# Sliding-window attention on one core: mixing with the values is issued behind the next half's scores, and the row maxima ahead of the output split

## The chip, the cores and the metric

The kernel runs on one core of a Trainium2 chip. The metric is the device time of one execution in microseconds (us). The core has a matrix engine (TensorE: PE for its matmuls, PEld for its weight loads), VectorE (DVE), ScalarE (ACT), GpSimd (POOL) and SyncE (SP), which issues the DMAs. Each engine runs its own list of instructions in order, and they meet only through semaphores.

## The reference, cut to what matters

The input is x (4 x 1024 x 512). First comes a banded cross-attention with a context (here "the band"), then two layers of a transformer block:

```python
for l in range(2):
    h = shift_token(x)
    q, k, v = split(h @ wqkv[l])               # 8 heads of 64
    q, k = rotary_xpos(l2norm(q) * qs, l2norm(k) * ks)
    o = local_attention(q, k, v)               # a row sees at most the 256 rows before it
    x = x + o @ wo[l]
    x = x + gated_ffn(layernorm(shift_token(x)))
```

For each row, local_attention takes the scores with the keys in reach, their maximum, the exponentials, divides by their sum, and multiplies with the values. All of it is in float32, which TensorE gets by splitting an operand into a rounded ("high") and a remaining ("low") part and making three products.

## The kernel before

The rows are cut into 32 tiles of 128 (8 per batch entry). The phases are the band, attention of layer 0, its FFN, attention of layer 1, its FFN. The change touches only the attention phase.

That phase is one software pipeline, written out by hand in five programs, one for each engine. Each has a loop `for s in range(TILES + 3)` and inside it two halves, `for d in (0, 1)`. In step s the tile t = s - 2 has its scores made (four heads in each half), tile s - 3 ("tail") is finished, tile s is projected to q, k and v, and tile s + 1 is turned (transposed). A tile reaches over 1, 2 or 3 tiles of keys: one for the first tile of a batch entry, two for the second, three for the other six (`reach`, L126).

TensorE's list for an inner step is, with the lines of its functions:

- d = 0: `scores(t, 0)` (L1074, matmuls L1094, six for each of two pairs of heads); the projection to the values (`project`, L976, matmuls L1000, twelve); `turn_probabilities(t - 1, 1)` (L1107, transposes L1116, twelve); eight more matmuls of the projection; `turn_h(s + 1)` (L1042, four transposes L897); `mix(t - 1, 1)` (L1120, L1133, 24 matmuls where the reach is three).
- d = 1: `scores(t, 1)`; ten matmuls of the projection; `turn_probabilities(t, 0)`; `project_out(tail)` (L1138, twelve matmuls L901 to L903); `turn_q` and `turn_k` of tile t + 1 (L1056, L1064); the last six matmuls of the projection; `mix(t, 0)`.

A half's probabilities are therefore turned one half later than its scores, and mixed at the end of that half. Three things hold the order together:

- PSUM banks. The four banks of `quad` are shared: the scores of the even pair of heads use banks 2 and 3, those of the odd pair banks 0 and 1. `turn_h` and `turn_q` write bank 1 and `turn_k` writes bank 0. So the odd pair in half d = 1 waits until h of tile s + 1 has been taken out of bank 1, which is L1088:

```python
w.wait_ge(S("hT_low"), base + min(t + 3 + d, TILES))
```

- Operands. `scores` starts with waits for both parts of q and k of its tile (L1080, L1081: qT_low, kT_low). These are made from PSUM by ACT (high, `copy` at L1354, called from `split_q`, `split_k`, `split_h`) and then DVE (low, L1718, functions of the same names).
- The lists of ACT and DVE. DVE takes the maxima (`maximum`, L1878, L1884), which also move the scores out of PSUM, scales the probabilities (`divide`, L1863), splits h, q and k, and splits the mixed output (`split_out`, L1921). ACT takes the exponentials (`probabilities`, L1528, L1533), copies turned probabilities (`copy_turned`, L1564), and makes the first part of the splits. In d = 1 both have `split_out(tail)` ahead of the maxima and of the exponentials. `turn_probabilities` waits at L1111 until all four maxima of the half just scored are taken, since it writes the same banks. `project_out` waits for oT_low, DVE's `split_out`.

POOL turns q and k by the rotary tables and scales some probabilities. In steps 12, 14, 16 and 18, DVE also has an extra scaling between `split_q` and `split_k` (`early_scale`, L2013, L2016), and in many steps POOL, ACT and DVE prepare parts of the FFN's weights (part_low, part_high).

Of the kernel before, what the change touches and what calls it, by code (L numbers as in the profile page):

```python
# [214 lines left out]
def build(nc, x, ctx, mask, wqkv, q_scale, k_scale, wo, ln_g, ln_b, w1, b1, w2, b2, consts, out):  # L215
# [676 lines left out]
    def tensor_program(e):  # L892
# [146 lines left out]
        def attend(l):  # L1039
# [80 lines left out]
            def mix(t, d):  # L1120

                n = base + t
                k, tiles, _, _ = reach(t)
                w.wait_ge(S("v_rows"), n + 1)
                w.wait_ge(S("oT_low"), n)
                if t == 0 and d == 0:
                    w.wait_ge(S("hT_low") if l else S("x1"), base + 2 if l else TILES)
                for turned, p in enumerate(duo(d)):
                    wait_copied(n, d, turned + 1)
                    for j in range(tiles):  # L1130
                        for i, half in enumerate(half_of):
                            h = 2 * p + i
                            ins = e.matmul(banks[5][half, p * P:(p + 1) * P],  # L1133
                                           A.v_rows[:, k - tiles + 1 + j, h * HD:(h + 1) * HD],
                                           A.probT[p % 2][:, i, j * P:(j + 1) * P], start=j == 0, stop=j == tiles - 1)
                    ins.then_inc(S("lmix"), 1)
# [14 lines left out]
            for s in range(TILES + 3):  # L1151
                t, tail = s - 2, s - 3
                live, ended = 0 <= t < TILES, 0 <= tail < TILES
                inside = 1 < s < TILES
                if s == 0:
                    turn_h(1)
                    project(l, 0, 0, 12)
                if s == 1:
                    project(l, 1, 12, 24)
                    turn_h(2)  # L1160
                    project(l, 1, 24, 36)
                    turn_q(0)
                    project(l, 1, 0, 6)
                    turn_k(0)
                    project(l, 1, 6, 12)
                for d in (0, 1):
                    turned = (t, 0) if d else (t - 1, 1)
                    mixing = 0 <= turned[0] < TILES
                    if live:
                        scores(t, d)  # L1170
                    if inside:
                        project(l, s, PROJECTED[d][0], PROJECTED[d][1])
                    if (s, d) == (TILES, 0):
                        project_out(tail - 1, 0)
                    if (s, d) == (TILES, 1):
                        turn_unit(l, 0)
                        turn_unit(l, 1)
                        project_out(tail, 0)
                    if (s, d) == (TILES + 1, 0):
                        turn_unit(l, 4)  # L1180
                        turn_unit(l, 5)
                    if (s, d) == (TILES + 1, 1):
                        up_first(l, 0, 0)
                    if mixing:
                        turn_probabilities(*turned)
                    if (s, d) == (2, 0):
                        turn_h(3)
                    if inside and d == 0:
                        project(l, s, PROJECTED[0][1], PROJECTED[0][2])
                    if d == 0 and 3 <= s < TILES - 1:  # L1190
                        turn_h(s + 1)
                    if (s, d) == (TILES, 0):
                        project_out(tail - 1, 1)
                    if (s, d) == (TILES + 1, 0):
                        turn_unit(l, 6)
                    if (s, d) == (TILES + 2, 0):
                        project_out(tail - 1, 1)
                    if d and ended and s not in (TILES - 1, TILES):
                        project_out(tail, 0)
                    if d and ended and s not in (TILES - 1, TILES + 1):  # L1200
                        project_out(tail, 1)
                    if d and 2 <= s <= TILES:
                        turn_q(s - 1)
                        turn_k(s - 1)
                    if (s, d) == (TILES, 1):
                        turn_unit(l, 2)
                        turn_unit(l, 3)
                    if inside and d:
                        project(l, s, PROJECTED[1][1], PROJECTED[1][2])
                    if mixing:  # L1210
                        mix(*turned)
                    if (s, d) == (TILES + 2, 0):
                        up_second(l, 0, 0)
                        up_third(l, 0, 0)
# [135 lines left out]
    def scalar_program(e):  # L1350
# [165 lines left out]
        def attend(l):  # L1516
# [56 lines left out]
            for s in range(TILES + 3):  # L1573
                t, tail = s - 2, s - 3
                live, ended = 0 <= t < TILES, 0 <= tail < TILES
                for d in (0, 1):
                    turned = (t, 0) if d else (t - 1, 1)
                    if l and (s, d) == (0, 0):
                        split_h(l, 1)
                    if d == 0 and rotated_tile(s) is not None and (l or s):  # L1580
                        square(l, rotated_tile(s))
                    if d and ended:
                        split_out(tail)
                    if live:
                        for h in range(4 * d, 4 * d + 4):
                            probabilities(t, h)
                    if (s, d) == (TILES + 1, 0):
                        split_unit(l, 4)
                        split_unit(l, 5)
                    if (s, d) == (TILES + 1, 1):  # L1590
                        keep_first(l, 0, 0)
                    if 0 <= turned[0] < TILES:
                        copy_turned(*turned)
                    if (s, d) == (TILES, 1):
                        split_unit(l, 0)
                        split_unit(l, 1)
                    if (s, d) == (TILES + 1, 0):
                        split_unit(l, 6)
                    if d == 0 and s < TILES and s != 1:
                        keep_v(s)  # L1600
                    if l and (s, d) == (0, 0):
                        e.activation(small[:, 0, 0:16], half_power[:, :], ACT.Exp).then_inc(S("half_power"), 1)
                    if d == 0 and 1 <= s < TILES - 1:
                        split_h(l, s + 1)
                    if l and (s, d) in ((0, 0), (1, 0)):
                        out_split_begin(l, 2 * s)
                        out_split_begin(l, 2 * s + 1)
                    if l and (s, d) == (2, 0):
                        attend_split_finish(l, 3)
                    if d and 1 <= s <= TILES:  # L1610
                        split_q(s - 1)
                        split_k(s - 1)
                    if (s, d) == (1, 1):
                        keep_v(1)
                    if prepared_item(s, 1) is not None:
                        if d:
                            round_parts(l, prepared_item(s, 1))
                        else:
                            round_sums(l, prepared_item(s, 1))
                    if (s, d) == (TILES, 1):  # L1620
                        split_unit(l, 2)
                        split_unit(l, 3)
                    if (s, d) == (TILES + 1, 0):
                        down_split_begin(l, 0)
                    if (s, d) == (TILES + 2, 0):
                        down_split_finish(l, 0)
                    if (s, d) == (TILES + 2, 1):
                        gate(l, 0, 0)
                        split_u(l, 0, 0)
                        down_split_begin(l, 1)  # L1630
# [77 lines left out]
    def vector_program(e):  # L1708
# [145 lines left out]
        def attend(l):  # L1854
# [66 lines left out]
            def split_out(t):  # L1921
                n = base + t
                w.wait_ge(S("oT_high"), n + 1)
                low(A.oT[:, 1, :], banks[5], A.oT[:, 0, :], S("oT_low"))
# [9 lines left out]
            for s in range(TILES + 3):  # L1934
                t, tail = s - 2, s - 3
                live, ended = 0 <= t < TILES, 0 <= tail < TILES
                for d in (0, 1):
                    early = early_tile(s) if d else None
                    if d and ended:
                        split_out(tail)  # L1940
                    if live:
                        for h in range(4 * d, 4 * d + 4):
                            maximum(t, h)
                    if (s, d) == (0, 0):
                        split_h(1)
                    if l and (s, d) == (0, 0):
# [488 lines left out]
```

## Time and profile before

| what | value |
|---|---|
| median of 3 runs | 2904.82 us (2904.49 to 2905.25) |
| the profiled execution | 2905.07 us |
| its span, first to last instruction | 2903.3 us |
| PE busy / PEld busy | 2872.9 us (99%) / 2526.7 us (87%) |
| DVE / ACT / POOL busy | 2075.6 us (71%) / 1340.3 us (46%) / 1328.4 us (46%) |
| mean granted TensorE clock | 1.000 |

The band takes about the first 220 us. Attention of layer 0 lies at about 220 to 850 us, that of layer 1 at about 1575 to 2210 us; the rest is FFN. A row of the timeline gives start, duration, engine, line, operation and tiles; equal neighbours are merged and counted with x; in brackets stands the idle time of the engine ahead of it and what ended it. A matmul's end is modelled and reaches over the start of the next, so for PE starts are compared with starts.

### The profile page before, as it was taken

How to read it: one execution, taken by the hardware profiler on the slowest of the kernel's cores; microseconds unless marked ns; L12 is line 12 of the kernel's file. 1: busy time of each engine (PE TensorE's matmuls, PEld its weight loads, DVE VectorE, ACT ScalarE, POOL GpSimd, SP SyncE). 2: the span in 40 equal slices, each digit the busy share in tenths (PEclk: the TensorE clock that was granted, in tenths of full speed). 3: DMA queues.
4: the chain of work that ended last, by engine and by line, in shares of the span. 5: the costliest groups of instructions: out<-in, count | busy, mean ns of one | idle time of the engine just before them, and what ended most of it. 6: DMA issues, size and time to landing. Idle time of an engine off the chain costs nothing. (4 is left out here: it accounts for less than half of the span.)

```text
span 2903.3 us, 53018 instructions
## 1 busy us (share of the span) xinstructions
PE 2872.9 (99%) x20256; PEld 2526.7 (87%) x20256; DVE 2075.6 (71%) x4135; ACT 1340.3 (46%) x2807; POOL 1328.4 (46%) x1406
## 2 busy tenths in 40 slices
PE   9999999999999999999999999999999999999999
PEld 7887888888889999999998887888888999999998
DVE  8987777776677666766657777776676766666765
ACT  7875556555554222222235555555555332222221
POOL 7767677776642211122105676766662222222221
PEclk9999999999999999999999999999999999999999
DMA  6753233322147777777783223332217777777775
GB/s 219 238 186 102 95 102 106 115 95 81 32 163 294 276 280 261 268 266 257 258 312 117 95 92 110 110 106 88 62 56 288 272 281 272 279 283 280 282 272 186
DMA packets 184897, 547.02 MB, mean 188 GB/s; under 512 B 26678, under 2 KB 82490, under 8 KB 162116
## 3 DMA queue, kind: packets, MB, share of 16 engines
q1 hardware_dynamic: 184500, 543.57, 52.9%
q8 instruction: 161, 2.64, 0.4%
q14 instruction: 92, 0.75, 0.1%
q10 hardware_dynamic: 144, 0.07, 0.0%
HBM read 447.11 MB, written 93.70 MB: 186 GB/s over the span
## 5 line engine op out<-in xcount | busy, mean ns | idle before, releaser
L1246 PE MATMUL quad<-fhT_f,slot_f 128*128 128x256 f32 (+1 forms) x2088 | 595.4, 285 | 0.2 <-DVE sums_f L2061 0.2
L1247 PE MATMUL quad<-fhT_f,slot_f 128*128 128x256 f32 (+1 forms) x2088 | 590.7, 283 | 0.0
L1248 PE MATMUL quad<-fhT_f,slot_f 128*128 128x256 f32 (+1 forms) x2088 | 590.5, 283 | 0.0
L1246 PEld LDWEIGHTS quad<-fhT_f,slot_f 128*128 128x128 f32 (+1 forms) x2088 | 392.9, 188 | 0.4 <-DVE sums_f L2061 0.4
L1248 PEld LDWEIGHTS quad<-fhT_f,slot_f 128*128 128x128 f32 (+1 forms) x2088 | 393.1, 188 | 0.0
L1247 PEld LDWEIGHTS quad<-fhT_f,slot_f 128*128 128x128 f32 (+1 forms) x2088 | 393.1, 188 | 0.0
L1665 ACT ACTIVATE gate_f_raw<-gate_f_raw,bias_f 128x512 f32<-128x512 f32 (+1 forms) x176 | 127.2, 722 | 552.2 <-DVE gate_f_raw L2084 552.2
L1533 ACT ACTIVATE lprob<-lprob,small 128x384 f32<-128x384 f32 (+2 forms) x512 | 288.5, 565 | 179.0 <-DVE small L1884 179.0
L2172 POOL TENSOR_SCALAR stats<-stats 128x1 f32<-128x1 f32 x64 | 35.6, 557 | 692.1 <-DVE stats L2024 691.3
L2289 POOL TENSOR_TENSOR turned_qk<-with_cos,with_sin 128x256 f32<-128x256 f32 x252 | 186.7, 761 | 337.6 <-DVE with_sin L1908 243.9
L1000 PE MATMUL bank_pair<-wqkv_h,hT 128*128 128x512 f32 x992 | 318.7, 402 | 0.0
L1884 DVE CUSTOM_DVE_ANT_0 lprob<-quad,far 128x384 f32<-128x384 f32 (+2 forms) x512 | 228.8, 503 | 74.6 <-PE quad L1094 74.6
L2280 POOL TENSOR_SCALAR lprob<-lprob,small 128x384 f32<-128x384 f32 (+2 forms) x192 | 238.7, 1250 | 23.7 <-DVE small L1869 23.7
L2346 POOL TENSOR_TENSOR res_f<-res_f,bias_f 128x512 f32<-128x512 f32 x63 | 89.2, 1416 | 282.5 <-DMA res_f<-stream 282.5
L2095 DVE SCALAR_TENSOR_TENSOR u_f<-sums_f,bias_f,gate_f_raw 128x512 f32<-128x512 f32 (+1 forms) x176 | 147.2, 837 | 95.6 <-ACT gate_f_raw L1665 95.6
L1354 ACT ACTIVATE lprobT<-quad 128x768 f32<-128x768 f32 (+2 forms) x256 | 172.2, 724 | 68.2 <-PE quad L1116 66.7
L1000 PEld LDWEIGHTS bank_pair<-wqkv_h,hT 128*128 128x128 f32 x992 | 177.5, 189 | 29.7
L1000 PE MATMUL bank_pair<-wqkv_l,hT 128*128 128x512 f32 x496 | 201.7, 407 | 0.0
L2207 POOL TENSOR_TENSOR norm<-norm,half_power 128x16 f32<-128x16 f32 x64 | 196.1, 3064 | 5.3
L1116 PEld LDWEIGHTS quad<-ident,lprob 128*128 128x128 f32 x1344 | 151.7, 141 | 32.8 <-DVE small L1884 20.4
L2084 DVE TENSOR_TENSOR gate_f_raw<-quad,sums_f 128x512 f32<-128x512 f32 (+1 forms) x174 | 120.3, 691 | 79.2 <-PE quad L1248 76.3
L1116 PE MATMUL quad<-ident,lprob 128*128 128x128 f32 x1344 | 169.4, 274 | 7.3 <-DVE small L1884 7.2
(296 smaller groups left out, 7344.1 us busy)
## 6 DMA issues: line engine op xcount, KB each, us to landing
slot_f<-parts SPq DMA_DIRECT2D x160, 1792.0 KB, 7.7
slot_f<-parts SPq DMA_DIRECT2D x16, 1190.0 KB, 5.2
s_in<-stream SPq DMA_DIRECT2D x128, 128.0 KB, 2.8
s_res<-stream SPq DMA_DIRECT2D x64, 256.0 KB, 2.8
stream<-a_out SPq DMA_DIRECT2D x64, 256.0 KB, 2.0
res_f<-stream SPq DMA_DIRECT2D x63, 256.0 KB, 7.3
h_in_f<-stream SPq DMA_DIRECT2D x112, 128.0 KB, 5.3
parts<-part_high SPq DMA_DIRECT2D x20, 512.0 KB, 2.6
```

Source lines behind the costliest of these rows:

```text
L1000: ins = e.matmul(bank, A.hT[n % 2][:, i % 2, c * P:(c + 1) * P], (wqkv_l if i == 2 else wqkv_h)[:, c, cols], start=(c, i) == (0, 0), stop= ...
L1116: ins = e.transpose(quad[:, pair_banks(p) + i, j * P:(j + 1) * P], A.prob[p][:, i, j * P:(j + 1) * P], ident[:, :])
L1246: e.matmul(bank[0:n, :], high, row_high, start=c == 0, stop=False)
L1247: e.matmul(bank[0:n, :], high, row_low, start=False, stop=False)
L1248: ins = e.matmul(bank[0:n, :], low, row_high, start=False, stop=c == 1)
L1354: return e.activation(to, source, ACT.Copy)
L1533: e.activation(prob, prob, ACT.Exp, bias=sm[:, h:h + 1], scale=-1.0, accum_out=sm[:, 8 + h:9 + h]).then_inc(S("lprob"), 1)
L1884: e.tensor_tensor_reduce(A.prob[h // 2][:, h % 2, 0:cols], quad[:, pair_banks(h // 2) + h % 2, 0:cols], A.far[:, WIN - cols:], 1.0, BIG, A ...
L2095: e.scalar_tensor_tensor(out=Fm.u[q % 2][0:n, :], in0=flat(Fm.sums[q % 2][0:n, 0:2, :]), scalar=Fm.bias1[0:n, 0, j:j + 1], in1=Fm.gate[q % ...
L2207: e.tensor_tensor(nm[:, 16:32], nm[:, 0:16], half_power[:, :], ALU.pow).then_inc(S("norm_inverse"), 1)
L2280: e.tensor_scalar(prob, prob, sm[:, 16 + 2 * p:17 + 2 * p], None, ALU.mult).then_inc(S("pscaled_pool"), 1)
L2289: e.tensor_tensor(turned[:, :, a:a + h2], cos[:, :, a:a + h2], sin[:, :, b:b + h2], ALU.add).then_inc(S("rotated"), 1)
```

## The change

On TensorE `mix` of both halves of tile t - 1 moves. The first half's, formerly at the end of the half d = 1 of step s, now stands in the half d = 0 of step s + 1 behind that half's scores. The second half's, formerly at the end of d = 0, stands behind the scores of d = 1 of the same step. The functions, waits and buffers are the same. On DVE `split_out` goes from ahead of the four maxima of d = 1 to behind them, and on ACT from ahead of the four exponentials of d = 1 to between the second and the third.

```diff
 # tensor_program, attend
                     mixing = 0 <= turned[0] < TILES
                     if live:
                         scores(t, d)
+                    if ended:
+                        mix(tail, d)
                     if inside:
                         project(l, s, PROJECTED[d][0], PROJECTED[d][1])
...
                     if inside and d:
                         project(l, s, PROJECTED[1][1], PROJECTED[1][2])
-                    if mixing:
-                        mix(*turned)
 # scalar_program, attend
-                    if d and ended:
+                    if d and ended and not live:
                         split_out(tail)
                     if live:
                         for h in range(4 * d, 4 * d + 4):
+                            if h == 6 and ended:
+                                split_out(tail)
                             probabilities(t, h)
 # vector_program, attend
-                    if d and ended:
-                        split_out(tail)
                     if live:
                         for h in range(4 * d, 4 * d + 4):
                             maximum(t, h)
+                    if d and ended:
+                        split_out(tail)
```

## Rows read from the trace of the kernel before

**Rows 1.** The page, busy time of each engine (share of the span, instructions)

```profile
PE 2872.9 (99%) x20256; PEld 2526.7 (87%) x20256; DVE 2075.6 (71%) x4135; ACT 1340.3 (46%) x2807; POOL 1328.4 (46%) x1406
```

**Rows 2.** Busy time by stretch: length, PE, PEld, DVE, ACT, POOL, clock, DMA share, GB/s

```profile
225.00:846.00 621.00, 612.94 (x4517) 501.82 (x4517) 452.44 (x1096) 362.87 (x832) 432.38 (x401) 1.00 0.29 95
1583.00:2209.00 626.00, 619.12 (x4597) 508.23 (x4596) 454.19 (x1094) 366.62 (x834) 425.37 (x393) 1.00 0.29 98
```

**Rows 3.** Waits of PE, whole span: total us, times, longest

```profile
PE quad L1116 <- DVE small L1884: 7.2, 23, 1.3
PE quad L1094 <- DVE hT L1718: 3.2, 10, 0.7
```

**Rows 4.** Timeline, layer 1, from turning h to the scores of d = 1

```profile
1713.95 0.60 PE L897 MATMUL quad<-ident,s_in 128*128 128x128 f32 x4
1714.47 1.53 PE L1133 MATMUL bank<-lprobT,v_rows 128*64 128x128 f32 x24
1714.58 0.60 ACT L1354 ACTIVATE hT<-quad 128x512 fp32r<-128x512 f32 x1 [0.93 <-PE quad L897]
1715.21 0.69 DVE L1718 TENSOR_TENSOR hT<-quad,hT 128x512 fp32r<-128x512 f32 x1 [0.40 <-ACT hT L1354]
1715.93 1.32 PE L1094 MATMUL quad<-kT,qT 64*128 64x384 f32 x12
```

**Rows 5.** Timeline, the same place one batch entry later, mixing of reach one

```profile
1752.67 0.66 PE L1133 MATMUL bank<-lprobT,v_rows 128*64 128x128 f32 x8
1753.25 0.62 PE L1094 MATMUL quad<-kT,qT 64*128 64x256 f32 x6
...
1753.40 0.69 DVE L1718 TENSOR_TENSOR hT<-quad,hT 128x512 fp32r<-128x512 f32 x1
1754.15 0.63 PE L1094 MATMUL quad<-kT,qT 64*128 64x256 f32 x6 [0.28 <-DVE hT L1718]
```

**Rows 6.** Timeline, scores of reach one in d = 1

```profile
1736.67 0.89 PE L1094 MATMUL quad<-kT,qT 64*128 64x128 f32 x12
```

**Rows 7.** Timeline, layer 1, from d = 1 into the next d = 0

```profile
1704.14 0.69 DVE L1718 TENSOR_TENSOR qT<-quad,qT 128x512 fp32r<-128x512 f32 x1 [3.16 <-ACT qT L1354]
...
1704.75 0.68 DVE L1718 TENSOR_TENSOR kT<-quad,kT 128x512 fp32r<-128x512 f32 x1
...
1705.23 1.53 PE L1133 MATMUL bank<-lprobT,v_rows 128*64 128x128 f32 x24
```

**Rows 8.** Timeline, layer 1, the same place after step 32

```profile
2183.96 1.53 PE L1133 MATMUL bank<-lprobT,v_rows 128*64 128x128 f32 x24
...
2185.02 0.68 DVE L1718 TENSOR_TENSOR kT<-quad,kT 128x512 fp32r<-128x512 f32 x1
...
2185.84 1.33 PE L1094 MATMUL quad<-kT,qT 64*128 64x384 f32 x12 [0.35 <-DVE kT L1718]
```

**Rows 9.** Line L2016: min/median/max ns, first and last start

```profile
L2016 DVE SCALAR_TENSOR_TENSOR square<-square,stats,shift x8: 743/748/1211, 434.5 to 1907.3; 128x512 f32<-128x512 f32 x8
```

**Rows 10.** Timeline, the last projection matmul ahead of turned probabilities, d = 0 and d = 1

```profile
1710.57 0.39 PE L1000 MATMUL bank<-wqkv_l,hT 128*128 128x512 f32 x1
1710.80 1.47 PE L1116 MATMUL quad<-ident,lprob 128*128 128x128 f32 x12
...
1719.36 0.39 PE L1000 MATMUL bank_pair<-wqkv_l,hT 128*128 128x512 f32 x1
1719.94 1.53 PE L1116 MATMUL quad<-ident,lprob 128*128 128x128 f32 x12 [0.20 <-DVE small L1884]
```

**Rows 11.** Timeline, layer 1, mixing followed by full-array transposes

```profile
2200.10 1.53 PE L1133 MATMUL bank<-lprobT,v_rows 128*64 128x128 f32 x24
2201.57 1.53 PE L1116 MATMUL quad<-ident,lprob 128*128 128x128 f32 x12
```

**Rows 12.** Timeline, layer 1, the last mixing and the split of its output

```profile
2204.41 1.53 PE L1133 MATMUL bank<-lprobT,v_rows 128*64 128x128 f32 x24
...
2206.61 0.69 DVE L1718 TENSOR_TENSOR oT<-bank,oT 128x512 fp32r<-128x512 f32 x1 [1.41 <-ACT oT L1354]
```

## The prediction

> **What bounds the kernel now.** I began with the page: PE is busy for 99% of the span, no other engine for more than 71% [rows 1]. The busy time by stretch says the same of both attention phases: 612.94 of 621.00 us and 619.12 of 626.00 us, at a granted clock of 1.00 [rows 2]. So TensorE's own list sets the time. A change of order takes away none of its work; it can only remove or make waits. Next I read PE's waits. What this change could remove is small: 7.2 us in 23 waits of the turned probabilities on DVE's maxima. And the second row of the group is a warning: scores already wait for h's split, 10 times, 3.2 us [rows 3]. So the question is what the moved mixing stands between, which only the timeline shows.
>
> **What the mixing hides now, d = 1.** In a full tile (reach three) the list is: turning h at 1713.95, mixing at 1714.47, scores at 1715.93 [rows 4]. Mixing thus takes 1.46 us between starts. Meanwhile ACT copies h (1714.58) and DVE splits it from 1715.21 to 1715.90 [rows 4]; both start within 0.03 us of their input, so this chain cannot be shorter. The odd pair's scores, which write h's bank, start half of 1.32 us after the even pair's, at 1716.59, and find it free. With mixing gone from there, the even pair starts at 1714.47 and the odd pair would at 1715.13. It must wait until 1715.90 and a release. That release took 0.06 us: DVE done at 1754.09, PE at 1754.15 [rows 5]. So 1715.96: a **new stall of 0.83 us**. It isn't paid back, since mixing then follows at its full length. Rows 5 are the natural experiment: mixing has reach one there and hides only 0.58 us (1752.67 to 1753.25), and the odd pair does wait. With it moved, the odd pair starts no earlier and mixing's 0.58 us is added behind. Where the scores have reach one, the odd pair is due after half of 0.89 us [rows 6], so its stall is 0.66 - 0.45 = 0.21 us longer, 1.04.
>
> Count: h is turned with a mixing behind it in steps 3 to 30, 28 in each layer. Of these 4 have the short mixing, 3 the narrow scores (tiles 8, 16, 24), 21 are ordinary: 4 x 0.58 + 3 x 1.04 + 21 x 0.83 = 22.9 us, for two layers **+45.7 us**.
>
> **The next d = 0.** Here scores need k's low part. DVE has it at 1704.75 + 0.68 = 1705.43, and mixing starts at 1705.23 [rows 7]; today its 1.46 us cover this. The release of the first pair took 0.14 us where it was the last thing waited for: 2185.70 to 2185.84 [rows 8]. So scores start at 1705.57 instead of 1705.23, **0.34 us late**. There are 31 such places in a layer, 62. Eight have the extra scaling between q and k, 0.75 us each [rows 9], so 1.09. After step 32 (two places) k comes even after the mixing, which is added in full, 1.46 [rows 8]. 52 x 0.34 + 8 x 1.09 + 2 x 1.46 = **+29.3 us**.
>
> **What it removes.** In d = 1 the turned probabilities wait for the fourth maximum: 0.58 us after the last projection matmul's start instead of 0.23 [rows 10], a loss of 0.35. With maxima first on DVE and 1.46 us of mixing more between scores and turning, this is gone: 23 x 0.35 = **-8 us**. Ends: nothing at all, and 20 us if each of the 23 lost nearly 0.9. I take 8, from the row. Next late behind them would be ACT's copy of the turned probabilities; the mixing that needs it is now later too.
>
> **The moved splits.** DVE's split_out no longer stands ahead of the maxima, and ACT's waits behind two exponentials. What hides this is the ten projection matmuls and the twelve transposes that stand between mixing and project_out, over 3.5 us (ten starts 0.23 apart and 1.47 [rows 10]). Split output is there 2.89 us after mixing's start (2204.41 to 2207.30), of which mixing is 1.46 [rows 12]; two exponentials more fit in the rest. I cost it at nothing. If that cover is gone, it is 1.49 us: 2.89 + 0.06 - 1.46. That happens at the end of each layer: the last mixing now stands directly ahead of project_out, behind two FFN products: 2 x 1.49. In step 32, only eight transposes stand between, two thirds of 1.47 us [rows 10]: 2 x 0.5. Together **+4.0 us**. No DMA moves past another in SP's list, and POOL's list is untouched.
>
> **Switches of the array's shape.** The three kinds of matmul use it whole, by rows (scores) and by columns (mixing). 24 mixings take 1.46 us and 8 take 0.58 [rows 4, 5]; 16 more thus cost 0.88, 0.055 each, and 0.14 us is left for the switch. Mixing ahead of whole-array work takes 1.47 us, 2200.10 to 2201.57 [rows 11], the same as ahead of scores. Scores directly ahead of mixing are nowhere in the trace. Bounds for that one: no switch cost (-0.14) to twice (+0.14), at 128 places -18 to +18 us. I take 0, since the measured pairs agree. The Trainium skill, page "TensorEngine Tiling (Array Packing)", section Key Properties, says that every change of tiling mode drains TensorE. A half has three changes before and three after, so by that rule, too, the estimate is no difference.
>
> **Sum.** 45.7 + 29.3 - 8 + 4 = +71 us on the profiled execution's 2905.07 us, which is 0.25 us above the median of the runs shown: **2976 us**.
>
> **The rivals.**
>
> One handover hurts only. If ACT and DVE come to q and k earlier in d = 1, k's 29 us fall away: 2905 + 46 + 4 - 8 = 2947 us. Against it: ACT and DVE already stood idle ahead of them (3.16 us of DVE before q [rows 7]), so they can't start earlier. Chance 0.06.
>
> DVE comes late. Its split_out now waits for ACT behind two exponentials, and `divide` behind it. If that pushed an instruction of 0.69 us in front of every k, 62 x 0.69 = 43 us more: 3019 us. It decides once the delay exceeds the 3.16 us of idle [rows 7]; I see some 1.5. Chance 0.07.
>
> The other side, faster. The waits on the maxima go, and the handovers stay hidden: 2905 - 8 = 2897 us. This needs h's chain from the start of turning to the free bank, 1.95 us now (1713.95 to 1715.90), to come down to 1.12, at which point the odd pair would wait no more. It consists of 0.60 us of transposes, 0.60 of ACT and 0.69 of DVE with nothing between [rows 4], so I give it 0.03.
>
> The change doesn't do what it says: some other wait already holds the mixing where it is now, 2905 us. But rows 4 show mixing starting 0.52 us after four transposes began, with no wait named. Chance 0.02.
>
> The clock falls. Both phases run at 1.00, though PE idles about 8 us in each [rows 2]. More and longer stalls could bring the granted clock to 1.2 GHz. For a tenth of 1247 us that would be 125 us of work taking twice as long: 3100 us. The Trainium skill, "TensorE: Matmul & The Clock Gate", section HAM oscillation, has a kernel in which TensorE's waits brought its clock down again and again. Those waits were for DMAs, and no run here shows the lower clock. Chance 0.01.
>
> My forecast has the remaining 0.81.
>
> **How the numbers follow.** Range, low end: switch free (-18), a release of 0.06 instead of 0.14 us for k (-5), the removed waits worth 20 instead of 8 (-12): 2976 - 35 = 2941. That takes in the first rival. High end: +18 for the switch, and a few late k's of the second rival's kind, +6: 3000. Left out are 0.07 + 0.03 + 0.02 + 0.01 and some tails of the forecast. A measurement of this kernel can tell about 0.2%, 6 us, from no change. Faster: 0.03. Same: 0.02. Slower: the rest, 0.95.
>
> **What the profile after would show.** Scores of d = 1 split in two groups of six, the second waiting for DVE's hT, in nearly all of steps 3 to 30, both layers: about 56 waits of PE on hT in place of 10. New waits of PE on kT, about 60. None on the maxima ahead of turned probabilities in d = 1. Both attention stretches about 35 us longer, with the same PE work; the band and the FFN unchanged. I am wrong if the odd pair starts less than 1.9 us after h's first transpose, or if the stretches don't grow.

## The result: 2.5% slower, two handovers uncovered

| | median us | runs |
|---|---|---|
| before | 2905.01 | 2904.49 to 2905.25 |
| changed | 2977.69 | 2977.16 to 2979.03 |

The ratio is 1.0251, with a 95% interval of 1.0238 to 1.0263. The forecast was 2976 us. The profiled execution took 2979.03 us, 74.0 us more than that of before.

The changed kernel's page has the same number of instructions on every engine, and a smaller busy share of PE (97%, from 99%); its row of before is [rows 1]:

```profile
PE 2887.0 (97%) x20256; PEld 2531.5 (85%) x20256; DVE 2066.5 (69%) x4135; ACT 1339.4 (45%) x2807; POOL 1337.6 (45%) x1406
```

Busy time by stretch (length, PE, PEld, DVE, ACT, POOL, clock, DMA share, GB/s), the same parts of the work as [rows 2]: 621 us became 658, and 626 became 663. All of the time was lost in the attention phases, 37 us in each.

```profile
225.00:883.00 658.00, 621.81 (x4531) 505.99 (x4530) 449.65 (x1105) 364.14 (x838) 437.03 (x401) 1.00 0.28 90
1620.00:2283.00 663.00, 626.67 (x4600) 511.71 (x4601) 449.78 (x1095) 366.12 (x835) 430.13 (x392) 1.00 0.28 93
```

PE's waits (total us, times, longest), against [rows 3]. The 10 waits on h have become 58. I read the 58 "issue" waits ahead of scores as those for k: the view names nothing for them, but they stand at the places where they were forecast, and in the half d = 0 shown below k lands just ahead of the scores. The waits on the maxima have left the list of PE's longest.

```profile
PE quad L1094 <- DVE hT L1720: 42.2, 58, 0.9
PE quad L1094 <- issue: 21.0, 58, 1.3
PE bank L901 <- DVE oT L1720: 4.7, 4, 1.4
PE quad L1094 <- DVE qT L1720: 3.5, 2, 1.8
```

The timeline of one half d = 1 of the changed kernel, layer 1, against [rows 4]. (DVE's lines are 2 higher than before, L1720 for L1718.)

```profile
1756.43 0.60 PE L897 MATMUL quad<-ident,s_in 128*128 128x128 f32 x4
1756.95 0.79 PE L1094 MATMUL quad<-kT,qT 64*128 64x384 f32 x6
1757.06 0.60 ACT L1354 ACTIVATE hT<-quad 128x512 fp32r<-128x512 f32 x1 [0.94 <-PE quad L897]
1757.69 0.69 DVE L1720 TENSOR_TENSOR hT<-quad,hT 128x512 fp32r<-128x512 f32 x1 [1.91 <-ACT hT L1354]
1758.44 0.79 PE L1094 MATMUL quad<-kT,qT 64*128 64x384 f32 x6 [0.69 <-DVE hT L1720]
...
1759.16 1.53 PE L1133 MATMUL bank<-lprobT,v_rows 128*64 128x128 f32 x24
...
1760.62 0.50 PE L1000 MATMUL bank_pair<-wqkv_l,hT 128*128 128x512 f32 x1
...
1763.06 1.47 PE L1116 MATMUL quad<-ident,lprob 128*128 128x128 f32 x12
```

This is the sequence that was forecast. The even pair starts 0.52 us after h's transposes; the odd pair stops until DVE is done (1757.69 + 0.69 = 1758.38) and starts 0.06 us later. From the first transpose to the odd pair it is 2.01 us, and 2.01 was forecast. ACT and DVE did not get faster, because both already started within 0.03 us of their input. At 1763.06 the turned probabilities start without a wait.

From h's first transpose to the first projection matmul behind mixing and scores it is 1760.62 - 1756.43 = 4.19 us. Before it was 1717.18 - 1713.95 = 3.23 us, the end of [rows 4] being:

```profile
1717.18 0.50 PE L1000 MATMUL bank_pair<-wqkv_l,hT 128*128 128x512 f32 x1
```

So the place costs 0.96 us, 0.13 more than the forecast stall of 0.83; why is told under h below.

In the next half d = 0, against [rows 7], k is ready at 1769.68 and scores start at 1769.78. The last projection matmul ahead of them had started at 1769.15, and without a wait scores follow such a matmul by 0.33 us (in the run with q and k turned earlier, below):

```profile
1769.00 0.68 DVE L1720 TENSOR_TENSOR kT<-quad,kT 128x512 fp32r<-128x512 f32 x1
1769.15 0.40 PE L1000 MATMUL bank_pair<-wqkv_l,hT 128*128 128x512 f32 x1
1769.78 0.88 PE L1094 MATMUL quad<-kT,qT 64*128 64x128 f32 x12 [0.23 <-issue]
```

### The profile page after: what moved, and what is told of

Same layout as the page of the kernel before. It is cut to its first block and busy times, and to the rows that moved or that the text cites. A ratio compares the mean times of both kernels' runs of the same rounds, so it can differ in the third digit from the quotient of the medians.

```text
span 2977.2 us, 53018 instructions
## 1 busy us (share of the span) xinstructions
PE 2887.0 (97%) x20256; PEld 2531.5 (85%) x20256; DVE 2066.5 (69%) x4135; ACT 1339.4 (45%) x2807; POOL 1337.6 (45%) x1406
## 5 line engine op out<-in xcount | busy, mean ns | idle before, releaser
L2282 POOL TENSOR_SCALAR lprob<-lprob,small 128x384 f32<-128x384 f32 (+2 forms) x192 | 231.1, 1210 | 59.7 <-DVE small L1871 59.0
L1094 PE MATMUL quad<-kT,qT 64*128 64x384 f32 (+2 forms) x1536 | 172.2, 342 | 68.0 <-DVE hT L1720 42.2
L1094 PEld LDWEIGHTS quad<-kT,qT 64*128 64x128 f32 x1536 | 121.2, 185 | 121.4 <-DVE hT L1720 58.4
L1720 DVE TENSOR_TENSOR qT<-quad,qT 128x512 fp32r<-128x512 f32 x64 | 44.2, 691 | 230.4 <-ACT qT L1354 230.4
```

The lines of the kernel that those rows point to most:

```text
L1094: ins = e.matmul(quad[:, pair_banks(p) + i, 0:cols], A.qT[n % 2][half, q_part, p * P:(p + 1) * P], A.kT[half, k_part, p, keys], start=q_pa ...
L2282: e.tensor_scalar(prob, prob, sm[:, 16 + 2 * p:17 + 2 * p], None, ALU.mult).then_inc(S("pscaled_pool"), 1)
```

## Experiments

All times are medians, with the runs of before made beside them on the same chip. "Gaps" are sums over both attention phases: by how much the distance between the starts of neighbouring matmuls exceeds its undisturbed value. A "stretch" is the whole time from the last matmul ahead of mixing and scores to the first one behind both.

### One half's mixing at a time

The second half's mixing behind the scores of d = 1 only, the splits as in the changed kernel:

```diff
-                    if ended:
+                    if ended and d:
                         mix(tail, d)
...
+                    if mixing and d:
+                        mix(*turned)
```

> The second half's mixing (tail, 1) stands behind the scores of d = 1 as in the changed kernel; the first half's stays at the end of d = 1, ahead of the next scores. Splits of ACT and DVE as in the changed kernel. Theory (two uncovered handovers, h and k, that add up; the waits on the maxima gone): h's stalls of 45.7 us stay, k's 29.3 us are gone, the ends' 4 us stay, the waits on the maxima stay away (-10): about 2905 + 46 + 4 - 10 = 2945 us, with 56 waits of PE on hT and no more than 5 on kT or on issue ahead of scores. Rival (the two share one slack, so that whichever mixing moves, the stall shows up at the other place): 2970 us or more.

Measured: 2957.98 us against 2905.62, ratio 1.0179 (1.0165 to 1.0193). PE's waits in it:

```profile
PE quad L1094 <- DVE hT L1722: 42.8, 58, 1.3
PE bank L901 <- DVE oT L1722: 7.4, 4, 2.3
```

The first half's mixing only:

```diff
-                    if ended:
+                    if ended and not d:
                         mix(tail, d)
...
+                    if mixing and not d:
+                        mix(*turned)
```

> The first half's mixing (tail, 0) stands behind the scores of d = 0 as in the changed kernel; the second half's stays ahead of the scores of d = 1. Splits as in the changed kernel. Theory: only k's handover is open: 2905 + 29 - 10 = 2924 us, up to 2930 with a small stall at project_out in the last step; about 58 new idle stretches of 0.2 to 0.4 us ahead of scores of d = 0, hT waits no more than about 10. Rival (shared slack): 2950 us or more. With the first run it tells whether the two terms add up: (first - 2895) + (second - 2895) should be the changed kernel's 2978 - 2895 = 83 us within 5.

Measured: 2937.67 us, ratio 1.0109 (1.0094 to 1.0125).

```profile
PE quad L1094 <- issue: 23.3, 58, 2.1
PE quad L1116 <- DVE small L1888: 5.7, 13, 0.5
...
PE quad L1094 <- DVE hT L1722: 2.7, 10, 0.3
```

Each stall came where its mixing was taken away, and not at the other place, so the rival of one shared slack falls. But the runs were 13 and 14 us above the forecast, and the sum that I had set as a test came to 63 + 43 = 106 us instead of 83. The 2895 us that I took as a base was wrong, as the next run shows.

### The splits alone

```diff
 # tensor_program: as before. scalar_program and vector_program: as in the changed kernel
```

> TensorE's list as before; only the splits of the output move behind the maxima on DVE and between the exponentials on ACT. Theory: the 23 waits of the turned probabilities on the maxima lose DVE's 0.68 us ahead of them and most of the 10 us that they cost (gaps over the usual 0.23 us, summed) go: 2895 to 2899 us, faster than both kernels, and project_out does not wait. Rival (the relief came from the mixing that now stands between scores and turning, not from the order on DVE): 2905 us, waits on the maxima as before. Other rival (the output is split too late for project_out): slower than 2905 us, with new waits of PE L901 on oT.

Measured: 2906.96 us against 2905.62, ratio 1.0003 (0.9994 to 1.0012). This was a **miss**: no gain. The gaps say why. Those at the turned probabilities fell from 10.2 to 0.3 us, as expected, but others grew. PE's waits:

```profile
PE bank L901 <- DVE oT L1720: 4.9, 4, 2.3
PE quad L1094 <- DVE kT L1720: 4.1, 8, 1.0
...
PE quad L1116 <- DVE small L1886: 2.5, 2, 1.2
```

Step 32 of layer 0 shows one of them. Only eight transposes stand there between scores and project_out:

```profile
826.69 0.60 ACT L1533 ACTIVATE lprob<-lprob,small 128x384 f32<-128x384 f32 x1
...
827.29 0.57 ACT L1354 ACTIVATE oT<-bank 128x512 fp32r<-128x512 f32 x1
...
827.90 0.69 DVE L1720 TENSOR_TENSOR oT<-bank,oT 128x512 fp32r<-128x512 f32 x1 [0.42 <-ACT oT L1354]
...
828.64 0.50 PE L901 MATMUL bank<-wo_h,oT 128*128 128x512 f32 x1 [2.28 <-DVE oT L1720]
```

Mixing had begun at 822.56 there, yet ACT copies its output only at 827.29, behind the second exponential, which itself waited for maxima. DVE stands idle 0.42 us for it, and PE 2.28. The three places that gave time back are step 32 (4.9 us of waits in two layers), scores whose q and k were split late (2.8 us), and project_out behind the short turnings (2.6 us).

With 2907 as the base, the single halves cost 51 and 31 us, and 50 and 29 were expected. Together that would be 82 us, and the changed kernel has 71. The two handovers themselves do add up. Summed over all stretches of mixing and scores, against the run with the splits alone, the second half's run has 52.6 us more, the first half's 30.5, together 83.1, and the changed kernel 82.4. The 11 us lie in other places. Most of them are the 13 waits on the maxima of the first half's run (shown above; 7.7 us by gaps), which neither this run nor the changed kernel has. At all 13, DVE splits parts of an FFN weight (`part_low`) ahead of the maxima, and takes 2.1 us for it (once 1.84). In this run the same instruction takes 1.23 us. First this run, then the first half's:

```profile
1714.43 1.23 DVE L1720 TENSOR_TENSOR part_low<-part_low_raw,part_high 128x1024 fp32r<-128x1024 f32 x1 [0.25 <-ACT part_high L1354]
```

```profile
1648.31 2.09 DVE L1722 TENSOR_TENSOR part_low<-part_low_raw,part_high 128x1024 fp32r<-128x1024 f32 x1 [0.25 <-ACT part_high L1356]
...
1652.36 1.53 PE L1116 MATMUL quad<-ident,lprob 128*128 128x128 f32 x12 [0.46 <-DVE small L1888]
```

In the changed kernel it takes 2.1 us too at these places, but 1.46 us of mixing stand there between scores and turning, and no wait is left. Some 2 to 3 us more are at project_out in step 32 (2.2 us in the changed kernel against 4.8 here).

### The mixing alone, splits as before

```diff
 # tensor_program: as in the changed kernel. scalar_program and vector_program: as before
```

> TensorE's list as in the changed kernel, splits of DVE and ACT as before, ahead of the maxima and exponentials of d = 1. Theory: DVE now stands still at split_out until the mixing behind the scores has ended and ACT has copied; the four maxima start about 2.9 us after the mixing's start and end 1.9 us later, about 0.9 us after the turned probabilities are due. 56 to 60 times 0.9: 2978 + 52 = 3030 us (3010 to 3040), with some 58 waits of PE L1116 on the maxima. Rival (the 1.46 us of mixing between scores and turning cover any order on DVE, so the moved splits cost and bring nothing): 2978 us.

Measured: 3028.03 us, ratio 1.0421 (1.0407 to 1.0435).

```profile
PE quad L1094 <- DVE hT L1718: 42.1, 58, 0.9
PE quad L1116 <- DVE small L1884: 41.1, 56, 1.0
```

So the two parts of the change belong together. With mixing behind the scores, a split ahead of the maxima makes DVE wait for work that PE has only just reached. The moved splits, ACT's and DVE's together, are worth 50 us in the new order and nothing in the old. No run tells how the 50 us divide between the two engines.

### Giving the handovers their cover back

If the stalls are missing cover, cover of any kind must close them, in proportion to its length, and not beyond their own. In the changed kernel, h was turned before the last 2, or the last 4, of the 8 projection matmuls of d = 0:

```diff
-                        project(l, s, PROJECTED[0][1], PROJECTED[0][2])
+                        project(l, s, PROJECTED[0][1], PROJECTED[0][2] - 2)     # or - 4
                     if d == 0 and 3 <= s < TILES - 1:
                         turn_h(s + 1)
+                    if inside and d == 0:
+                        project(l, s, PROJECTED[0][2] - 2, PROJECTED[0][2])     # or - 4
```

> The changed kernel, with h turned before the last 2 of the 8 projection matmuls of d = 0 instead of behind them. Theory (the stall is the part of h's handover that nothing covers): 2 x 0.23 = 0.46 us of cover more at 56 places, so -25.5 us: 2952 us, each wait on hT about 0.4 us instead of 0.85. Rival (the wait is set by DVE's or ACT's own lists and not by when h is turned): 2978 us, waits on hT as before.

> The changed kernel, with h turned before the last 4 of the 8 projection matmuls. Theory: 0.91 us of cover more than close the 0.85 us: h's term of about 49 us is gone, 2978 - 49 = 2929 us, waits on hT no more than about 10. Beyond the dose of 0.85 us nothing more comes. Rivals: 2978 us if the other lists set it; between 2935 and 2955 us if the turning of h now waits itself for ACT's copy of the turned probabilities in its bank.

Measured: 2951.18 us with two, 2925.21 with four (before: 2905.20). That is 26.5 and 52.5 us less than the changed kernel, where 25.5 and 49 were expected. So the time follows the cover. The 3.5 us above 49 belong to the stall as well (see h below). These two runs alone don't show the limit, as 0.91 us of cover is too near to the stall of 0.85; the last run of the next section does. PE's wait on h with two matmuls, then with four:

```profile
PE quad L1094 <- DVE hT L1722: 16.4, 58, 0.7
```

```profile
PE quad L1094 <- DVE hT L1722: 1.7, 4, 0.8
```

Third, q and k were turned two projection matmuls earlier as well:

```diff
-PROJECTED = ((0, 12, 20), (20, 30, 36))
+PROJECTED = ((0, 12, 20), (20, 28, 36))
```

> As the run before, and q and k turned before the last 8 of the projection matmuls instead of the last 6 (8 ahead of turned probabilities in d = 1 instead of 10). Theory: 0.46 us of cover more than the 0.31 us that k's handover lacks: some 50 x 0.31 + 8 x 0.45 = -19 us more, 2910 us. What is left against the kernel before is the last step's 3 us, step 32 and the extra scaling, so this order can at best draw level. Rival (k's term is something else, such as the switch of the array from whole to rows ahead of mixing): 2929 us.

Measured: 2910.33 us, ratio to before 1.0017 (1.0008 to 1.0026). PE's waits:

```profile
PE quad L1094 <- issue: 7.2, 8, 1.3
```

15 us more are gone, where 19 were expected; that the total is the expected 2910 us is luck, since h's part had given 3.5 us too much. Of 58 waits 8 are left, those with the extra scaling between q and k. So cover alone gave back 67 of the 73 us, and with it restored the new order still has no advantage over the old.

### A version that beats both

The run with the splits alone suggested taking only DVE's half of it, and that not in step 32. ACT's copy stays ahead of the exponentials, where in the old order the mixed output is already complete:

```diff
 # vector_program of the kernel before; nothing else
-                    if d and ended:
+                    if d and ended and s == TILES:
                         split_out(tail)
                     if live:
                         for h in range(4 * d, 4 * d + 4):
                             maximum(t, h)
+                    if d and ended and s != TILES:
+                        split_out(tail)
```

> The kernel before with one change: DVE's output split behind the four maxima of d = 1 (not in step 32); ACT's list and TensorE's as before. Theory: in the run with both splits moved, the 10 us of waits on the maxima went but 12 us came back, at project_out in step 32 (4.9), ahead of scores where q and k were split late (2.8) and at project_out behind short turnings (2.6), because ACT's copy of the output came behind two exponentials and DVE stood at it. With ACT's copy first again, the split is ready when DVE comes to it: 2905.6 - 10 = 2896 us, at most 2 us given back. Rival (DVE's part alone is late for k and project_out): 2903 to 2908 us.

Measured: 2894.65 us (2893.91 to 2895.04) against 2905.20, ratio **0.9964** (0.9951 to 0.9976), 10.5 us faster than the kernel before and 83 us faster than the changed one. PE's waits and one half d = 1 of it:

```profile
PE quad L1094 <- DVE hT L1718: 3.2, 10, 0.6
PE quad L1116 <- DVE small L1884: 3.0, 4, 1.2
...
PE quad L1094 <- DVE kT L1718: 1.4, 4, 0.4
```

```profile
1712.12 0.55 DVE L1884 CUSTOM_DVE_ANT_0 lprob<-quad,far 128x384 f32<-128x384 f32 x1
...
1712.60 0.69 DVE L1718 TENSOR_TENSOR oT<-bank,oT 128x512 fp32r<-128x512 f32 x1
1712.99 1.47 PE L1116 MATMUL quad<-ident,lprob 128*128 128x128 f32 x12
```

The split follows the last maximum at once, with no idle time ahead of it, the turned probabilities start without the wait of [rows 10], and project_out has no wait on oT. Against the run with the splits alone two things differ, ACT's list and step 32, and no run separates them; by that run's gaps step 32 is worth 4.9 us and ACT's list the other 5.4.

Last, h two projection matmuls earlier in this kernel, with the same edit to TensorE's list as above:

> The kernel of the run before (only DVE's split moved), and h turned before the last 2 of 8 projection matmuls. In that order mixing covers h's handover except at the 8 places with the short mixing, where 0.27 us was left open. Theory: 0.46 us of cover more close them and nothing else gains: 8 x 0.27 = -2 us, 2892.5 us, and no gain at the 48 places where the handover was covered already. Rival (each earlier turning gains its 0.46 us wherever it is made): 2869 us.

Measured: 2894.67 us, the same. That falsifies the rival, and it shows the limit: 0.46 us of cover more at 48 places that were covered already brought nothing. But the 2 us didn't come either. The waits on h went from 10 to 4, and PE waited 1.6 us less for them:

```profile
PE quad L1094 <- DVE kT L1720: 1.8, 5, 0.4
PE quad L1094 <- DVE hT L1720: 1.6, 4, 0.7
```

In exchange, nine gaps ahead of scores have 2.7 us, 1.0 more than without. What took the rest stays open; it is at the limit of what can be measured.

## Why the prediction was right

Term by term, against the profiled execution of the changed kernel. The gaps are those at the wait itself; a stretch, where given, holds everything between the matmuls around mixing and scores:

| term | forecast | gaps, changed less before | stretches, changed less before |
|---|---|---|---|
| h's handover, 56 places | +45.7 | +46.3 | +51.2 |
| k's handover, 60 places, and k after step 32, 2 places | +29.3 | +31.0 | +24.8 and +5.4 |
| waits on the maxima | -8 | -10.2 | |
| project_out, last step and step 32 | +4.0 | +5.2 | |

**h.** Right in place, count and mechanism, and the wait is right in size: an ordinary one is 0.85 us (0.83 forecast), a narrow one 1.03 (1.04). But the forecast took the stall as the whole cost, and it isn't: the ordinary place costs 0.96 us. Behind a wait the odd pair takes 0.72 us until mixing starts (1758.44 to 1759.16); in the kernel before it took 0.62 until the projection. Where nothing waits, both pairs take 1.28 us, 0.64 each, as in the run with four matmuls of cover:

```profile
1703.64 1.35 PE L1094 MATMUL quad<-kT,qT 64*128 64x384 f32 x12
1704.92 1.53 PE L1133 MATMUL bank<-lprobT,v_rows 128*64 128x128 f32 x24
```

These 0.08 us at each stall also account for the 52.5 us of that run, where 49 were expected. The edited cover (two and four matmuls) shows the cause: 0.46 us at 56 places gave 26.5 us.

**k.** Right, 0.31 us at the ordinary place instead of 0.34. The eight places with the extra scaling have 1.1 to 1.4 us (1.09 forecast). The first-half run is no clean measure of this term, as its 31 us over the splits alone hold 7.7 us of waits on the maxima and lack some 5 us of waits around step 33.

**The maxima.** Right to go, at 10 instead of 8 us. What I had named only as part of the reason is that the splits must move too: without that, 50 us are lost.

**The moved splits, costed at nothing.** Right for the changed kernel, wrong as a general statement. The cover that I named (ten projection matmuls and twelve transposes) is shorter in step 32 and behind short turnings, and it is late for k where there is extra scaling. Step 32 came to 1.07 us a place and not 0.5. In the old order the late splits cost as much as they brought (10.3 us of gaps against 9.9).

**The switch of the array's shape, taken as no difference.** Right. Scores to mixing, which the trace of before did not have, takes 0.265 us between starts at full reach, the same as scores to the projection before; mixing to the projection takes 0.20, as mixing to scores did. The Trainium skill, page "TensorEngine Tiling (Array Packing)", section Key Properties, says that changing the tiling mode drains TensorE, and makes no difference between pairs of modes; the trace agrees, 0.265 us for both pairs that start from scores and 0.20 for both that start from mixing.

**The rivals.** "One handover hurts only" (2947 us) and "DVE comes late" (3019 us) did not happen: in the changed kernel DVE stood idle 3.47 us ahead of q's split, longer than the 3.16 us of [rows 7]. The clock's fall, which I gave one in a hundred, did happen, in miniature (below).

**What I did not see, and luck.** Around step 33 of each layer PE used to wait for maxima and for the FFN's first units (1.25 and 0.78 us in layer 1 of before). These places lost 4.7 us of gaps, since the later scores wait anyway; the scores of d = 1 there cost 1.2 us more. With h and k by stretches it is 51.2 + 30.2 - 10.2 + 5.2 - 4.7 + 1.2 = 72.9 of the 74.0 us; the rest is open. The lower clock, some 2 to 3 us, is in the 5.4. So the mechanism was right, and the miss of under 2 us is partly luck: h's term was 5.5 us too small, and the unseen 4.7 us and the 2 us more from the maxima made up for it.

## What to carry to other kernels

In a software pipeline at 99% of its bounding engine, a piece of work on that engine can also be the cover of a handover between its neighbours. Before moving it, list what is handed over across its old place and how long the way through the other engines takes. Here each such way that was longer than what remained became a stall of the difference, once for every repetition (0.85 us of wait and 0.96 us of time, where the difference was 0.83). If a wait on another engine's queue is the aim, reorder that queue first (here one DVE instruction in all steps but one, -10.5 us) and leave an engine's copy where its input is already complete.

## What the runs showed of the hardware

The granted clock did fall. Busy time by short stretches of the changed kernel, layer 1, around the start of step 33 (the clock is the third number from the end):

```profile
2251.00:2254.00 3.00, 3.00 (x21) 2.42 (x20) 1.68 (x4) 3.00 (x7) 0.26 (x1) 1.00 0.39 162
2254.00:2258.00 4.00, 2.23 (x25) 1.77 (x25) 3.96 (x9) 0.92 (x2) 2.43 (x2) 0.96 0.16 57
2257.70:2261.00 3.30, 3.30 (x28) 2.97 (x25) 1.95 (x9) 2.60 (x9) 0.00 (x0) 0.50 1.00 321
2261.20:2264.20 3.00, 2.49 (x25) 2.25 (x25) 2.59 (x6) 2.94 (x6) 0.14 (x1) 1.00 0.91 378
```

and the timeline of the same place:

```profile
2256.05 1.31 PE L1094 MATMUL quad<-kT,qT 64*128 64x384 f32 x12 [1.77 <-DVE qT L1720]
2257.30 2.52 PE L1133 MATMUL bank<-lprobT,v_rows 128*64 128x128 f32 x24
2259.75 1.12 PE L1232 MATMUL bank_pair<-ident,first_sums_f 128*128 128x128 f32 x4
```

PE waited 1.77 us for q, and was busy for 2.23 of 4 us. Then the clock stood at 0.50, which is 1.2 GHz, and the 24 mixing matmuls took 2.45 us between starts instead of 1.46; right after it was 1.00 again. The same happened at this place of layer 0, again behind a wait of 1.77 us for q; there these 24 took 2.66 us. So the mixing alone lost 1.0 and 1.2 us. Before, PE waited 0.35 us here [rows 8], and the clock was 1.00 (2180 to 2190 us). The Trainium skill, page "TensorE: Matmul & The Clock Gate", section HAM oscillation, ties such falls to longer waits for DMAs; here it came after a wait for another engine, the longest of PE in that phase. The 56 stalls of some 0.85 us did not bring the clock down.

The wait alone does not settle it. In the run with the mixing alone PE waits the same 1.77 us for q, in both layers, and the clock stays at 1.00. In layer 0:

```profile
893.00:896.00 3.00, 1.23 (x12) 0.95 (x12) 2.93 (x9) 1.35 (x3) 2.69 (x2) 1.00 0.00 0
896.00:899.00 3.00, 3.00 (x41) 2.58 (x38) 3.00 (x9) 1.31 (x5) 0.00 (x0) 1.00 0.79 223
```

The run with h, q and k turned earlier has this wait in both layers, and the clock fell in layer 0 only. Behind a wait of 2.3 us for oT in step 32 it fell in both layers of the second half's run, and in neither layer of the run with the splits alone. What decides is open.

DVE slowed down beside POOL. The split `part_low<-part_low_raw,part_high` (128x1024) occurs 20 times. It took 1.22 to 1.23 us each time in the kernel before and in the runs with the second half's mixing, the splits alone or DVE's split alone. In the changed kernel 13 of the 20 took 2.07 to 2.11 us, and in the first half's run 13 took 1.84 to 2.11 us. The other seven of each took 1.22 to 1.36 us. Beside each of the 26 slow ones, and beside none of the others, POOL ran `turned_qk<-with_cos,with_sin`; so the moved mixing of the first half had shifted the two lists against each other. Where q and k were turned earlier, all 20 took 1.37 us or less again. POOL lost too: the pair that takes 1.42 us in the run with the splits alone takes 2.43 in the first half's run. What the two engines share no run shows.
